# One group of attention heads, in an order written out by hand: row-maximum pieces spread over the key tiles, denominators behind V, and a bank's own last use as its wait

## What is computed

```
q = rope(x @ wq); k = rope(x @ wk); v = x @ wv
scores = q @ k.T / sqrt(32), masked above the diagonal
out = softmax(scores) @ v
x = x + out @ wo
```

## Time and profile before

| | |
|---|---|
| median of 3 runs | 3102.75 us |
| the profiled execution | 3104.36 us |
| its span in the profile | 3102.6 us |
| TensorE busy | 2783.3 us, 90% |
| VectorE busy | 1809.5 us, 58% |
| ScalarE busy | 1001.0 us, 32% |
| GpSimd busy | 716.3 us, 23% |
| mean granted clock of TensorE | 0.947 |

### The profile page before, as it was taken

How to read it: one execution, slowest core, us unless ns; L and a number is a source line. 1 busy time by engine, 2 the same in 40 slices (tenths; PEclk the granted TensorE clock), 3 DMA queues, 4 the chain that set the end, 5 groups by cost and what they waited for, 6 DMA issues and landing times. The chain is left out here.

```text
span 3102.6 us, 49549 instructions
## 1 busy us (share of the span) xinstructions
PE 2783.3 (90%) x15824; PEld 1790.7 (58%) x15824; DVE 1809.5 (58%) x4485; ACT 1001.0 (32%) x1549; POOL 716.3 (23%) x705
## 2 busy tenths in 40 slices
PE   7899998999999799652859999989999997997999
PEld 6555554655554488652646455446555543885887
DVE  5566767556666333588764666664666663225443
ACT  2234435134343411352521434433244344101000
POOL 7223231432231000000044323214223220001111
PEclk9999999999999899765979999989999998998999
DMA  4313221323231422000233313223323222433111
GB/s 147 105 55 98 61 82 62 114 77 93 62 97 34 138 81 68 0 0 0 81 118 108 108 54 96 63 71 105 93 65 96 62 74 85 151 134 146 68 68 41
DMA packets 121064, 252.84 MB, mean 81 GB/s; under 512 B 12720, under 2 KB 39728, under 8 KB 120880
## 3 DMA queue, kind: packets, MB, share of 16 engines
q1 hardware_dynamic: 120912, 251.03, 25.6%
HBM read 166.57 MB, written 84.41 MB: 81 GB/s over the span
## 5 line engine op out<-in xcount | busy, mean ns | idle before, releaser
L561 ACT ACTIVATE a_prob<-a_pst 128x1024 f32<-128x1024 f32 (+3 forms) x768 | 592.9, 813 | 728.4 <-PE a_pst L832 726.9
L648 DVE CUSTOM_DVE_ANT_0 a_psh<-a_psh,a_edge 128x128 f32<-128x128 f32 (+3 forms) x1024 | 488.0, 514 | 228.5 <-PE a_psh L785 218.5
L785 PE MATMUL a_psh<-a_kst,a_qst 127*128 127x512 f32 (+3 forms) x1536 | 514.4, 397 | 22.4 <-issue 7.1
L785 PEld LDWEIGHTS a_psh<-a_kst,a_qst 127*128 127x128 f32 x1536 | 258.3, 191 | 448.2 <-DVE a_mx L648 196.9
L832 PE MATMUL a_pst<-a_qst,a_kst 128*128 128x512 f32 (+2 forms) x1536 | 401.9, 363 | 25.8 <-DMA a_qst<-rowmax 9.7
L651 DVE TENSOR_REDUCE a_mx<-a_psh 128x1 f32<-128x512 f32 x512 | 343.8, 689 | 69.7 <-PE a_psh L785 63.5
L852 PE MATMUL a_ppv<-a_prob,a_vg 128*32 128x512 f32 (+3 forms) x3072 | 335.3, 509 | 14.6 <-POOL a_prob L465 8.0
L832 PEld LDWEIGHTS a_pst<-a_qst,a_kst 128*128 128x128 f32 x1536 | 269.6, 194 | 126.2 <-issue 59.9
L465 POOL TENSOR_SCALAR_AFFINE_SELECT a_prob<-a_prob 128x512 f32<-128x512 f32 x256 | 162.4, 634 | 757.7 <-ACT a_prob L561 757.4
L852 PE MATMUL a_pden<-a_prob,a_ones 128*32 128x512 f32 (+3 forms) x3072 | 333.2, 506 | 0.0
L433 POOL TENSOR_TENSOR a_swp<-a_swp,a_sin 128x512 f32<-128x512 f32 x80 | 103.7, 1296 | 337.9 <-DVE a_swp L637 325.5
(11 more groups left out here) (219 smaller groups left out, 4020.6 us busy)
## 6 DMA issues: line engine op xcount, KB each, us to landing
a_qst<-q SPq DMA_DIRECT2D x192, 256.0 KB, 4.5
a_wraw<-in_wqkv SPq DMA_DIRECT2D x52, 512.0 KB, 5.6
q<-a_stg_hi SPq DMA_DIRECT2D x64, 256.0 KB, 2.1
q<-a_stg_lo SPq DMA_DIRECT2D x64, 256.0 KB, 2.4
oT<-a_oT SPq DMA_DIRECT2D x64, 256.0 KB, 2.5
a_kst<-kT SPq DMA_DIRECT2D x96, 128.0 KB, 3.0
h_oraw<-oT SPq DMA_DIRECT2D x16, 512.0 KB, 4.1
h_x<-in_x SPq DMA_DIRECT2D x16, 512.0 KB, 4.7
```

The lines of the kernel that those rows point to most:

```text
L561: act.activation(prob[k % 2][:, 2 * half:2 * half + 2, off:], pst[:, half, :, off:], ACT.Exp, scale=scale).then_inc(s["exp_done"], 1)
L648: part = dve.tensor_tensor_reduce(scores, scores, edge[:, BANK - n:], 1.0, 2 * MASKED, ALU.add, ALU.max, mx_hq[kc][:, h, qt:qt + 1])
L785: mm = pe.matmul(psh[:, at, i * n:(i + 1) * n], qst[par][0:P - 1, h, qt * P:(qt + 1) * P], kst[par][0:P - 1, kc * BANK:kc * BANK + n], sta ...
```

## The change

The list of steps is no longer computed but written out as text (`ORDER`) and read by `parsed`. Against the old list:

- Half 0 of the projection begins before the first ST (four pieces), the other four stand among ST 0 and ST 1.
- S 0 stands between the two halves of ST 0, S 1 before V 0, and so on to S 37, between pieces of the second projection in unit 11. Before, the first three stood around V 1 and D 1.
- In units 0, 1, 2, 3, 10 and 11, D stands right behind V, or behind the next V. V 5 comes ahead of ST 6.
- MT stands behind six pieces of the second projection, not two. WL comes first on SyncE, then RS 1; HI 1 and LO 1 move behind the first ST steps. VG is a step at the end.
- `bank_plan` takes the last uses of the banks over from the group before, so the first use in a group waits for its own bank only. The plan is settled over two alternating groups.

The same list without some steps serves groups 7 and 8.

```diff
-def columns(step):
-    what, e, _ = step
-    n = BANK - unit_offset(e)
-    return 2 * max(n, BANK // 2) if what == "ST" else 4 * n
+ORDER = """
+    P:0.0 P:0.1 P:0.2 P:0.3
+    ST:0.0 WL S ST:0.1 P:0.4 P:0.5 HI:1 P:0.6
...
+    ST:11.0 ST:11.1 P:1.0 P:1.1 S P:1.2 P:1.3 P:1.4 P:1.5 MT NORM:0 P:1.6 V:10 V:11 D:10 RK D:11 P:1.7
+      NORM:1 VG
+"""
...
 def iteration(full_s=True, proj=True, ahead=False):
-    steps = [[("ST", e + 1, 0), ("ST", e + 1, 1), ("PV", e, 0), ("PV", e, 1)] for e in range(NU)]
...
-    if full_s:
-        window = [step for unit in steps[1:10] for step in unit]
-        total, done, k = sum(map(columns, window)), 0, 0
-        for step in window:
-            done += columns(step)
-            while k < len(USES) and k * total < done * len(USES) - total // 2:
-                after[step] += [("S", k)]
-                k += 1
...
+    left_out = set() if proj else {"P", "WL", "WS", "RK", "VG"}
+    if not full_s:
+        left_out |= {"S", "MT"}
+    order = []
+    for step in STEPS:
+        what, k = step[:2]
+        if what in ("HI", "LO", "RS") and not (proj if k == 0 else full_s):
+            continue
+        if what not in left_out:
+            order.append(step)
...
-def bank_plan(order, spare=()):
+def bank_plan(order, banks, spare=(), carried=None):
-    last, plan, n, held = {}, {}, 0, None
+    last, plan, n, held, used = dict(carried or {}), {}, 0, None, 0
...
-    return plan, n
+    return plan, n, {x: at - n for x, at in last.items()}
...
+    plan, kept, settled = {}, None, False
+    while not settled:
+        first = kept
+        for order in bodies:
+            plan[id(order)], U_IT, kept = bank_plan(order, (0, 1), carried=kept)
+        settled = first == kept
...
-                    group(body, b, j * 2 + par, j, par, u0 + (j * 2 + par) * U_IT)
+                    group(bodies[par], b, j * 2 + par, j, par, u0 + (j * 2 + par) * U_IT)
```

More of the change, by code:

```diff
@@ L74 @@
 PIECES = 8
-def columns(step):
-    what, e, _ = step
-    n = BANK - unit_offset(e)
-    return 2 * max(n, BANK // 2) if what == "ST" else 4 * n
-def iteration(full_s=True, proj=True, ahead=False):
-    steps = [[("ST", e + 1, 0), ("ST", e + 1, 1), ("PV", e, 0), ("PV", e, 1)] for e in range(NU)]
[L90 to L105, removed]
-    if full_s:
-        window = [step for unit in steps[1:10] for step in unit]
-        total, done, k = sum(map(columns, window)), 0, 0
-        for step in window:
-            done += columns(step)
-            while k < len(USES) and k * total < done * len(USES) - total // 2:
-                after[step] += [("S", k)]
-                k += 1
-        assert k == len(USES)
-        after[steps[10][1]] += [("MT", 0)]
-    after[steps[10][1]] += [("NORM", 0)]
@@ new lines @@
+ORDER = """
+    P:0.0 P:0.1 P:0.2 P:0.3
+    ST:0.0 WL S ST:0.1 P:0.4 P:0.5 HI:1 P:0.6
+    ST:1.0 LO:1 ST:1.1 P:0.7 S V:0 D:0
+    ST:2.0 S ST:2.1 S V:1 D:1 S HI:0
+    ST:3.0 RS:1 LO:0 ST:3.1 S V:2 D:2 RS:0 S
+    ST:4.0 S ST:4.1 S V:3 D:3
+    ST:5.0 S ST:5.1 S V:4 S D:4 S S V:5 S
+    ST:6.0 S ST:6.1 S WS D:5 S S
+    ST:7.0 S ST:7.1 S V:6 S S D:6 S
+    ST:8.0 S S ST:8.1 S V:7 S S D:7 S
+    ST:9.0 ST:9.1 S V:8 S S D:8 S
+    ST:10.0 ST:10.1 S V:9 S D:9 S
+    ST:11.0 ST:11.1 P:1.0 P:1.1 S P:1.2 P:1.3 P:1.4 P:1.5 MT NORM:0 P:1.6 V:10 V:11 D:10 RK D:11 P:1.7
+      NORM:1 VG
@@ new lines, with parsed @@
+"""
+def parsed(text):
+    steps, k = [], 0
+    for word in text.split():
+        what, _, rest = word.partition(":")
+        if what == "S":
+            steps.append(("S", k))
+            k += 1
+        elif what in ("ST", "P"):
+            steps.append((what, *(int(x) for x in rest.split("."))))
+        elif what in ("V", "D"):
+            steps.append(("PV", int(rest), "VD".index(what)))
+        else:
+            steps.append((what, int(rest or 0)))
+    assert k == len(USES)
+    return steps
@@ L117, in iteration, with put @@
+STEPS = parsed(ORDER)
+def iteration(full_s=True, proj=True, ahead=False):
+    left_out = set() if proj else {"P", "WL", "WS", "RK", "VG"}
[8 more added lines that the diff above has]
+            order.append(step)
     if ahead:
+        def put(step, *others):
+            order[order.index(step) + 1:order.index(step) + 1] = others
+        for i in range(PIECES):
+            put(("ST", 11, 1) if i < 6 else ("PV", 10, 0), ("P", "next", i))
@@ L120, in iteration @@
         for i in range(ST_):
[L121 to L132, removed]
+            put(max([("ST", i + 1, 0)] + [("XN", i - 2)] * (i > 1) + [("XC", i - 4)] * (i > 3), key=order.index), ("XS", i))
+            put(max(("PV", i, 0), ("XS", i), key=order.index), ("XN", i))
+            put(max([("ST", i + 3, 1), ("XN", i)] + [("XC", i - 1)] * (i > 0), key=order.index), ("XT", i))
+            late = max(("PV", i + 2, 0), ("XT", i), key=order.index)
@@ new lines, in iteration @@
+            put(late, ("XC", i), *[("XL", i + NX_AHEAD)] * (i + NX_AHEAD < ST_))
+        pieces = iter(range(PIECES))
+        order = [("P", "next", next(pieces)) if step[0] == "P" else step for step in order]
+        order = [("XL", i) for i in range(NX_AHEAD)] + order
+        for i in range(ST_):
+            assert sorted(("XS", "XN", "XT", "XC"), key=lambda w: order.index((w, i))) == ["XS", "XN", "XT", "XC"]
+            assert i == 0 or order.index(("XC", i - 1)) < order.index(("XC", i))
@@ L135, in prologue @@
+    return order
 def prologue():
@@ L174, in bank_plan @@
         if what == "P" and step[-1] == 0:
-            held = spare[len([k for k in plan if k[0] == "P"]) % len(spare)] if spare else \
-                min((0, 1), key=lambda x: last.get(x, -1))
+            held = spare[used % len(spare)] if spare else min(banks, key=lambda x: last.get(x, -1))
+            used += 1
             plan[step[:-1]] = [None, held, last.get(held, -1)]
@@ L182, in bank_plan @@
         if what in ("S", "MT", "VT"):
-            bank = min((x for x in (0, 1) if x != held), key=lambda x: last.get(x, -1))
+            bank = min((x for x in banks if x != held), key=lambda x: last.get(x, -1))
             plan[step] = [n, bank, last.get(bank, -1)]
@@ L212, in attention @@
     ZT0, W0, SH0, R0, E0, PV0, AC0, N0, ST0, DMA0 = 4, 2, 1, 4, 2, 2, 2, 1, 2, 16
-    pro, body, body6, body7 = prologue(), iteration(), iteration(proj=False), iteration(False, False)
+    pro, bodies, body6, body7 = prologue(), (iteration(), iteration()), iteration(proj=False), iteration(False, False)
     ahead7 = iteration(False, False, True)
-    plan_pro, U_PRO = bank_plan(pro, spare=(2, 3, 4, 5))
-    plan = {id(order): bank_plan(order)[0] for order in (body, body6, body7, ahead7)}
-    U_IT, U_IT6 = bank_plan(body)[1], bank_plan(body6)[1]
+    plan_pro, U_PRO, _ = bank_plan(pro, (0, 1), spare=(2, 3, 4, 5))
+    plan, kept, settled = {}, None, False
[4 more added lines that the diff above has]
+        settled = first == kept
+    plan[id(body6)], U_IT6, kept = bank_plan(body6, (0, 1), carried=kept)
+    plan.update({id(order): bank_plan(order, (0, 1), carried=kept)[0] for order in (body7, ahead7)})
     U_BATCH = U_PRO + 6 * U_IT + U_IT6 + 1
@@ L469, in group @@
                         reciprocal_deviation((b + 1) * ST_ + e, e)
-                if order is body:
-                    pool.wait_ge(s["pv_done"], PV0 + n * NU + NU)
-                    copy_v(b, g + 2, par)
+                    if what == "VG":
+                        pool.wait_ge(s["pv_done"], PV0 + n * NU + NU)
+                        copy_v(b, g + 2, par)
             pool.memset(ident[:, :], 0.0)
```

## The result

The changed kernel takes 3192.43 us (median of four runs, 3187.14 to 3196.35), the kernel before beside it 3101.25 (3098.82 to 3106.19). The ratio is 1.029, its 95% interval 1.027 to 1.031: 91 us slower; the forecast was 3180, 79 us slower. The profiled execution has a span of 3191.5 us and a mean granted clock of 0.928; it was 3102.6 and 0.947.

The account below looks back on a forecast made before the run. TensorE was taken to bound settled groups (busy 52.83 of 52.94 us). To 3104.4 us came 22 for waits net of savings and 57 for clock loss: 3183, rounded to 3180 as the runs' median is 1.6 lower; range 3125 to 3212.

Parts of the forecast that it names:

- Run price: TensorE, each separate run of V and D matmuls: 0.29 us; 22 runs become 17, 1.45 us less per full group.
- Bank waits, 0.6 us less: TensorE waiting for VectorE to free score banks: spreading the pieces saves 0 to 1.2 us a group, middle 0.6.
- Key wait of 2.4 us: In front of S 0, groups 2 to 6: keys land 8.9 us behind MT, TensorE's work ahead lasts 6.5.
- Group 1 and group 7: Group 1: S 0 keeps its place, waiting for queries, about 12 us; group 7: S 0 waits until 8.9 us behind MT.
- Clock: Granted clock falls behind standstills: 1.7 us for each of 2.4 us, 2.9 in groups 1 and 7; +57 us in all.
- rival 1: Behind the 2.4 us standstills at S 0 the clock holds: 34 us less, 3146 us; chance 0.12.
- rival 2: Behind the 2.4 us standstills the clock falls for the full stretch every time: 24 us more, 3204 us; chance 0.10.
- The stretch as a whole: From S 0 of group 1 to the first ST of group 8: 364.2 us per batch before 14.3 of clock loss.
- Group 8, the step that failed: Group 8, behind the stretch that was summed: the prediction gave it no cost.

Follow-up runs that it names:

- keys_first: The changed kernel with one step moved: key stacking (RK) right behind the group's last ST, ahead of the row-maximum round trip and output store; 3097.47 us (0.999).
- s0_back: The changed kernel with its first pieces put back, S 0 to S 3 behind V 0 and D 0, S 4 to S 6 in unit 3; 3098.4 us (0.999).
- runs_apart: `s0_back` with five joined runs of V and D cut apart by neighbouring pieces, 22 runs as before; 3108.35 us (1.003).
- banks_only: The kernel before with its computed list of steps and only the new bank plan; 3098.86 us (1.000).
- s0_front: The kernel before with only S 0 moved, between the two halves of the first ST; 3199.26 us (1.032).

## Why the prediction came out

It was right in sign, mechanism and place, and 12 us short. One term was missing, what group 8 costs. Step by step:

- **Run price.** 0.29 us forecast; 0.26 in busy time when five runs are cut apart again. Right.
- **Bank waits, 0.6 us less.** The undisturbed group of `keys_first` has 50.85 us for 50.9. Within the changed kernel S 0 to MT takes 44.54 us at full clock (725.19 to 769.73) for 44.4. Right as a sum here, and lucky: which kernel waits 0.2 and which 0.9 us depends on how the pieces lie, as `s0_back` and `runs_apart` show.
- **Key wait of 2.4 us.** 61.8 us in all for the keys, 14 of them in the four groups 7: 2.4 in each of the twenty (1.65 to 2.71). The keys were there 8.2 to 9.2 us behind MT, forecast 8.9. Right.
- **Group 1 and group 7.** S 0 to the next first ST in group 1: 53.16 us (135.29 to 188.45), forecast 50.4 + 2.9 = 53.3. Group 7: S 0 8.80 behind MT, 47.85 us from there to the first ST of group 8 (467.80 to 515.65), forecast 44.4 + 2.9. That S 0 keeps its place held: behind the prologue's MT it starts after 24.3, 24.8, 23.9 and 24.0 us, before after 24.1, 23.4, 24.2 and 23.9. The 2.35 us by which it is earlier in the first batch come from the prologue, which the change does not touch: its MT stands at 113.50 before, and with the old order of the groups too it stands at 111.24 in `banks_only` and 110.69 in `s0_front`. So it is a difference between executions. The wait itself was put too high, about 12 us for 7.8 to 9.8; with nothing moved ahead of S 0 but itself, in `s0_front`, it is 11.6 to 11.8. The sum does not depend on it, only on where S 0 starts.
- **Clock.** 1.7 us for a fall forecast. Two groups with the same wait, 2.26 with and 2.25 us without a fall, take 54.84 and 53.33: 1.5. It fell at 19 of 20, against rival 1. The cold stretch of 6.8 us of rival 2 came three times.
- **The stretch as a whole.** 380.36, 377.30, 377.49 and 379.62 us; forecast 364.2 + 14.3 = 378.5. Together they are 79.9 us more than before, where 22 + 57 = 79 were forecast. That it agrees to 1 us is partly luck: the bank waits and the clock were each a middle of a range.
- **Group 8, the step that failed.** The prediction costed it at nothing without a row for it; it did not look at the steps XN and XC at all. From the first ST of group 8 to the next S 0 the first batch of each layer takes 154.53 and 156.39 us instead of 150.00 and 150.30, the two stretches behind the second batches 0.2 and 0.5 more: 11.3 in sum. With the 2.35 us at the start, 79.9 + 11.3 - 2.35 comes to the difference of the spans, 88.9. Of the 10.6 us in the first batches, 6.7 are waits in front of the transposes (8.2 us where 1.5 were), and putting that pair of steps back took 11.0 from `s0_back` by the medians, about 5 by the traces.

The Trainium skill's page "TensorE: Matmul & The Clock Gate", section on HAM oscillation, tells of a matmul loop that waits about 3 to 5 us for a transfer in every pass and starts every pass cold. The prediction applied this to standstills of 2.4 us, which are shorter than the waits in the page's case, so that the page did not settle the question. The trace did: behind waits of 1.65 to 2.71 us the clock fell at 19 of 20, against rival 1. How often it falls depends on more than that. In `s0_front` it fell at two of ten waits of 1.05 to 1.80 us and at seven of ten of 1.86 to 2.26 us, and in both kernels most of the cold stretches behind such waits were 3.4 us long, not 6.8.

## What to carry to other kernels

A step that is moved forward takes its waits with it: before moving it, measure how long ahead its inputs arrive now (here 7.8 us of cover) and where their transfer stands on its queue. Issuing that transfer earlier cured as much here as moving the step back (3097 and 3104 us against 3098); in a settled group it gave more (50.85 us against 51.83), but it left the wait for the queries in group 1. The two cures were not tried together with the old list for group 8. Where one engine is full, shorter work on it can come back in part as waits for a second one that is busy for two thirds of the time: about half of what the joined runs save, in each of the three placings tried. And an order that serves several kinds of groups has to be read for each kind: the one that was not read cost about 10 us.

## What the runs showed of the chip beyond that

Where the clock falls behind a standstill of 2.3 us in otherwise full work, it costs 1.5 us more (54.84 us for 53.33), in a stretch of mostly 3.4 us at a granted clock of 0.50. Ten matmuls on old data in its place avoid that (clock 1.00, 43 us over the program). A standstill of the same length does not always do it. In `s0_front` the clock held at 2.12 and 2.16 us and fell at 2.08 and 2.10; first S 0 of two of these groups, then the granted clock behind it (third from last):

```profile
191.37 0.66 PE L786 MATMUL a_psh<-a_kst,a_qst 127*128 127x128 f32 x4 [2.08 <-DMA a_kst<-kT]
1817.85 0.66 PE L786 MATMUL a_psh<-a_kst,a_qst 127*128 127x128 f32 x4 [2.12 <-DMA a_kst<-kT]
...
192.28:195.69 3.41, 3.41 (x11) 2.74 (x10) 1.58 (x9) 1.54 (x2) 2.61 (x4) 0.50 0.20 77
1817.85:1821.26 3.41, 3.41 (x17) 2.96 (x18) 2.39 (x10) 2.03 (x3) 2.71 (x4) 1.00 0.20 77
```

What decides between them these runs do not tell.
